# Turning the last layer of a four-layer image kernel: channels on the partitions

## The reference, cut to what matters

```
def _L3_conv_ref(X, Ws, Wm, bm):            # X = _gn(x), L(v, i) = v @ Ws[i-1]
    ...
    ret = L(X, 10) + L(X.transpose(0, 2, 1, 3), 11)
    ret = ret + (L(sum_of_rows, 6) + L(sum_of_cols, 8) + L(diag_part, 12))[:, :, None, :]
    ret = ret + (L(sum_of_rows, 7) + L(sum_of_cols, 9) + L(diag_part, 13))[:, None, :, :]
    ret = ret + 2.0 * L(sum_diag_part, 14)[:, None, None, :]
    ...
    ret = ret + diag_term[:, :, None, :] * eye[None, :, :, None]
    return jax.nn.relu(ret @ Wm + bm)
...
x = x + _L3_conv_ref(_gn(x), L3_conv_Ws, L3_conv_Wm, L3_conv_bm)
```

## Time and profile before

| | |
|---|---|
| median of 3 runs | 1138.73 us (1138.61 to 1141.44) |
| the profiled execution, its span | 1140.7 us |
| busy over the span: PE, DVE, ACT, POOL | 92%, 67%, 43%, 35% |
| end of layer 2 to the first instruction of the block of layer 3 | about 1081.9 to 1086.08 us |
| from there to the first of 16 steps on DVE | 12.7 us |
| 16 steps on DVE | 1098.74 to 1138.25 us |

### The profile page before, as it was taken

One profiled execution on the slowest core, in us unless ns is written; L12 is line 12 of the kernel. 1 busy time (PEld: TensorE's weight loads), 2 busy tenths in 40 slices (PEclk: granted clock), 3 DMA queues, 4 the chain that ended last, 5 costly groups with the idle time before them and its releaser, 6 DMA issues. The chain is left out here.

```text
span 1140.7 us, 25192 instructions
## 1 busy us (share of the span) xinstructions
PE 1047.0 (92%) x9258; PEld 761.3 (67%) x9258; DVE 761.1 (67%) x3620; ACT 490.8 (43%) x1083; POOL 402.6 (35%) x545
## 2 busy tenths in 40 slices
PE   5888999999998699669999999999999999999788
PEld 3435888888887243347677776777777777777576
DVE  3684888888887332366767667676676766766268
ACT  2384777777776100224343343433434343343200
POOL 0153666666665100012232333323233232332331
PEclk8797999999999799769999999999999999999979
DMA  8000000000000000000000000000000000000012
GB/s 171 1 0 2 2 3 3 2 4 2 3 3 2 1 1 1 10 0 1 1 2 1 2 1 1 1 1 2 1 1 2 1 1 1 1 1 1 1 41 111
DMA packets 10317, 11.02 MB, mean 10 GB/s; under 512 B 3668, under 2 KB 8020, under 8 KB 10196
## 3 DMA queue, kind: packets, MB, share of 16 engines
q1 hardware_dynamic: 8820, 8.84, 3.0%
q10 hardware_dynamic: 1376, 0.59, 0.3%
HBM read 5.14 MB, written 4.19 MB: 8 GB/s over the span
## 5 line engine op out<-in xcount | busy, mean ns | idle before, releaser
L1591 PE MATMUL quad<-theta,nat 128*128 128x512 f32 x512 | 240.8, 593 | 0.0
L734 POOL TENSOR_TENSOR nat<-nat,arena 128x512 f32<-128x512 f32 x128 | 131.5, 1049 | 43.7 <-DVE arena L792 39.9
L1599 PEld LDWEIGHTS quad<-flat 128*128 128x128 f32 x768 | 104.7, 190 | 54.5 <-ACT flat L1397 31.7
L1599 PE MATMUL quad<-flat 128*128 128x128 f32 x768 | 123.7, 284 | 9.5 <-ACT flat L1397 9.5
L1591 PEld LDWEIGHTS quad<-theta,nat 128*128 128x128 f32 x512 | 87.5, 191 | 61.7 <-issue 61.7
L792 DVE CUSTOM_DVE_ANT_0 nat<-quad,arena 128x128 f32<-128x128 f32 x512 | 111.2, 283 | 1.9 <-PE quad L878 1.9
L1397 ACT ACTIVATE flat<-quad 128x256 f32<-128x256 f32 x192 | 73.4, 382 | 75.2 <-PE quad L1599 60.5
L751 ACT ACTIVATE nat<-bank 128x512 f32<-128x512 f32 x128 | 73.0, 597 | 65.5 <-PE bank L886 65.5
L1358 POOL COPY img<-flat 64x256 f32<-64x256 f32 x64 | 25.3, 395 | 193.9 <-DVE nat L1502 178.0
L886 PE MATMUL bank<-const,nat 128*128 128x128 f32 x512 | 73.3, 276 | 8.7 <-ACT nat L751 8.0
L756 ACT ACTIVATE nat<-nat 128x512 f32<-128x512 f32 x128 | 77.2, 634 | 4.7 <-POOL nat L734 4.7
(11 more groups left out here) (391 smaller groups left out, 2338.6 us busy)
## 6 DMA issues: line engine op xcount, KB each, us to landing
out<-nat SPq DMA_DIRECT2D x16, 256.0 KB, 2.0
const<-in_constants ACTq DMA_DIRECT2D x1, 400.5 KB, 3.2
arena<-in_L_conv_Ws SPq DMA_DIRECT2D x1, 240.0 KB
flat<-arena SPq DMA_DIRECT2D x3, 32.0 KB, 4.4
nat<-in_x SPq DMA_DIRECT2D x4, 0.2 KB, 12.1
arena<-in_L_conv_Wq ACTq DMA_DIRECT2D x1, 32.0 KB, 6.5
arena<-in_L_conv_Wk ACTq DMA_DIRECT2D x1, 32.0 KB, 6.3
arena<-in_L_conv_Wv ACTq DMA_DIRECT2D x1, 32.0 KB, 6.0
```

The source lines that it names most:

```text
L734: pool.tensor_tensor(scored, scored, of_head(least[b], h).broadcast_to([128, ROWS, L]), ALU.subtract).then_inc(lowered, 1)
L1591: return pe.matmul(m.quad[:, n, :], vT[:, col(n)], m.theta[:, part, :], start=(part == 0), stop=False, skip_group_check=True)
L1599: last = pe.matmul(m.quad[:, row, place * C:(place + 2) * C], a8[g % 2][:, col(row)], zs[half][k % 2][:, n, :], start=False, stop=(k == 2) ...
```

## The change

The layout of layer 3 is turned. Channels are on the partitions, of even columns j in partitions 0 to 63 and of odd ones in 64 to 127; rows i lie along the free axis. `mix` (128 x 64) is the stationary operand and the image the moving one, 512 columns at a time. What hangs on j is then a scalar of each partition, what hangs on i a row. The result is turned back at the end by transposes. In the order of the program:

- `group_norm` gets `sp_aside`: eight transfers from SBUF to SBUF on SP's queue, which copy partitions 0 to 63 of `img` (x itself) to the free tile `flat`, even columns to its lower half and odd ones to its upper half. `raw_rows` on DVE gets two copies, two sums and a scaling more; `sums_of_cols` on POOL drops two operations and clears `diag_pair`.
- The splitting, the three transfers, POOL's conversions and the products with ones are gone, and so are the diagonal tiles.
- The small sums are now 18 matmuls of 128 columns and 12 of one column, with 64 x 64 stationary pieces (before: 15 of 64 columns, two small ones for `both`).
- A step: PE makes 2 matmuls of 512 columns into one of four banks (`mixed`, each into one half of the partitions); DVE 4 scalar_tensor_tensor of 128 columns, then one small tensor_tensor of 128 x 8 on the diagonal; ACT the relu in place; POOL adds x (`residual(t)`, 128 x 512); PE turns the tile by 4 transposes (`turn`); ACT copies it to SBUF; SP sends it. The tiles `work` form a ring of 6, the outgoing ones a ring of 4.

The core of the diff:

```diff
+            for dst, src, landed in sp_aside:
+                sp.dma_start(dst, src).then_inc(landed, 16)
...
+    PARTS = ((0, 2), (2, 6), (6, 11), (11, 16))
+    residual_loads = [(m.flat[halves[q], first * CH:end * CH].rearrange("p (s i) -> p s i", i=L),
+                       stacked[halves[0], first * HALF:end * HALF, q, :], image_in[n])
+                      for n, (first, end) in enumerate(PARTS) for q in range(2)]
...
-    group_norm(nc, m, 3, pool_aside=sums_of_cols, dve_aside=raw_rows)
+    group_norm(nc, m, 3, pool_aside=sums_of_cols, dve_aside=raw_rows, sp_aside=residual_loads)
...
         @block.gpsimd
-            pool.wait_ge(S("flattened"), 16 * 3)
             for t in range(STEPS3):
-                pool.tensor_copy(m.parts[t % 2][:, :], s_flat[:, t * COLS * C:(t + 1) * COLS * C]).then_inc(parts_ready, 1)
+                pool.wait_ge(bent, t + 1)
+                pool.tensor_tensor(w, w, residual(t), ALU.add).then_inc(x_added, 1)
...
         @block.vector
-                dve.tensor_tensor(by_col(before[b]), result(b)[:, :, 0:C], of_row.unsqueeze(1).broadcast_to([128, COLS, C]),
-                                  ALU.add).then_inc(added, 1)
-                dve.tensor_tensor(before[b][own, :], before[b][own, :], diag_tile[t % 4][own, :], ALU.add).then_inc(added, 1)
-                dve.scalar_tensor_tensor(out=by_col(ready[b]), in0=by_col(before[b]), scalar=0.0, in1=result(b)[:, :, C:2 * C],
-                                         op0=ALU.max, op1=ALU.add).then_inc(out_ready, 1)
+                for s in range(HALF):
+                    last = dve.scalar_tensor_tensor(out=w[:, at], in0=m.quad[:, t % 4, at], scalar=of_col[:, t * HALF + s:t * HALF + s + 1],
+                                                    in1=of_row, op0=ALU.add, op1=ALU.add)
+                dve.tensor_tensor(own, own, diag_pair[:, t * HALF:(t + 1) * HALF, :], ALU.add).then_inc(added, 1)
...
+        @block.scalar
+            def keep(t):
+                act.wait_ge(turned, t + 1)
+                if t >= 4:
+                    act.wait_ge(sent[t % 4], 16 * (t // 4))
+                act.activation(ready[t % 4], turned_bank[t % 4][:, :], ACT.Copy).then_inc(out_ready, 1)
+            for t in range(STEPS3 + 3):
+                if t < STEPS3:
+                    act.wait_ge(added, 2 * t + 2)
+                    act.activation(work[t % RING], work[t % RING], ACT.Relu).then_inc(bent, 1)
+                if t >= 3:
+                    keep(t - 3)
...
         @block.tensor
+            def mixed(t):
+                for q in range(2):
+                    last = pe.matmul(m.quad[halves[q], t % 4, :], mix, stacked[:, t * HALF:(t + 1) * HALF, q, :],
+                                     start=True, stop=True, skip_group_check=True)
+            for t in range(0, STEPS3, 2):
+                turn(t)
+                turn(t + 1)
+                for later in (t + 4, t + 5):
+                    if later < STEPS3:
+                        mixed(later)
```

More of the change, by code:

```diff
@@ L8 @@
 F32 = mybir.dt.float32
-BF16 = mybir.dt.bfloat16
 ALU = mybir.AluOpType
@@ L1743, in layer3 @@
[L1743 to L1746, removed]
-    S = lambda name: m.sem(f"l3_{name}")
-    B = m.bank
-    kind = lambda k: w[:, (k - 1) * C:k * C]
-    by_col = lambda t: t.rearrange("p (j x) -> p j x", j=COLS)
+    HALF = COLS // 2
+    RING = 6
+    wm, bm = m.k3_wm, m.k3_bm
+    mix_raw, mix = m.take(C), m.take(C)
@@ new lines, in layer3 @@
+    raw, seen = (m.take(3 * L, C) for _ in range(2))
+    rows_raw, cols_raw, diag_raw = (raw[:, n * L:(n + 1) * L] for n in range(3))
+    rows_x, cols_x, diag_x = (seen[:, n * L:(n + 1) * L] for n in range(3))
+    mean_raw, mean = m.take(3, C), m.take(4, C)
+    col_half = m.take(L)
+    of_row, of_col, level = m.take(L), m.take(L // 2), m.take(2)
+    diag_pair = m.take(L).rearrange("p (s q) -> p s q", q=2)
+    nat_tiles = iter(m.nat[:, n:n + CH] for n in range(0, L * C, CH))
+    work = [next(nat_tiles) for _ in range(RING)]
@@ new lines, in layer3, with residual @@
+    ready = [next(nat_tiles) for _ in range(4)]
+    B = m.bank
+    totals, diag_totals = B[0], B[1]
+    turned_bank = [B[2], B[3], B[0], B[1]]
+    halves = (slice(0, C), slice(C, 128))
+    kind = lambda k: m.k3_w[:, (k - 1) * C:k * C]
+    by_col = lambda t: t.rearrange("p (s x) -> p s x", s=HALF)
+    stacked = m.img[:, 0:L * L].rearrange("p (s q i) -> p s q i", q=2, i=L)
+    def residual(t):
+        return m.flat[:, t * CH:(t + 1) * CH]
+    S = lambda name: m.sem(f"l3_{name}")
+    image_in = [m.sem(f"image_part_in_{n}") for n in range(4)]
@@ L1822, in _ @@
-            dve.wait_ge(terms_made, 4)
-            dve.tensor_copy(diag_term, B[0][:, 0:C]).then_inc(S("diag_ready"), 1)
-            dve.wait_ge(S("diag_ready"), 1)
-            step(lay_diag(dve, 0))
+            step(dve.tensor_copy(level[:, 1:2], diag_totals[:, L:L + 1]))
+            for q in range(2):
+                last = dve.tensor_scalar(diag_pair[halves[q], :, q], diag_totals[halves[q], q:L:2], level[halves[q], 1:2], None, ALU.add)
+            last.then_inc(prepared, 1)
+            dve.wait_ge(prepared, 4)
@@ new lines, in _ @@
+            last.then_inc(terms_made, 1)
+            for q in range(2):
+                total(diag_totals, q, column(0), [(kind(1), diag_x), (kind(3), rows_x), (kind(4), cols_x)])
+            for q in range(2):
+                last = total(diag_totals, q, slice(L, L + 1), [(kind(2), mean[:, 1:2]), (kind(5), mean[:, 0:1])])
+            last.then_inc(terms_made, 1)
+            for t in range(1, 4):
+                mixed(t)
+            for t in range(0, STEPS3, 2):
[4 more added lines that the diff above has]
+                        mixed(later)
@@ L1894, in _ @@
-            for b in range(2):
-                sp.wait_ge(sent[b], 16 * STEPS3 // 2)
+                sp.dma_start(out.rearrange("b i j c -> (b i) j c")[:, t * COLS:(t + 1) * COLS, :],
+                             ready[t % 4].rearrange("p (j c) -> p j c", c=C)).then_inc(sent[t % 4], 16)
+            for n in range(4):
+                sp.wait_ge(sent[n], 16 * (STEPS3 // 4))
 def build(nc, args, out):
```

152 lines of the change are left out of this document (56 added, 96 removed).

## The result

The changed kernel takes 1147.57 us (median of 6 runs, 1145.14 to 1152.26), the kernel before 1138.67 us in the same comparison (6 runs, 1137.71 to 1141.44). The ratio is 1.0074 with an interval of 1.0056 to 1.0092, so the change costs 6.4 to 10.5 us. The profiled execution has a span of 1144.1 us.

A forecast was written before the change was run, and what follows sets the result against it. PE was taken to bound the steps at 2.30 us each. Span 1140.7 plus 10.0 of delay less 5.3 gained gives 1145.4 us, and with the profiled span 2.0 above the median, 1143.4 us; range 1133 to 1149.

The forecast's parts named there:

- The delay: Last block's start: SP hands over eight transfers before the barrier, so it begins 10 us later, ends 4.5 to 13.4.
- the seam: Norm of layer 3 up to the last block's first instruction: 4 us before, to be lengthened by SP's hold.
- The price per run: Eight copies ahead of the barrier: a cost per run and byte, 28 ns for 512 bytes, gives 10.4 us.
- Rival 2: At the barrier: SP doesn't hold the block, issues cost 0.64 us each, time 1134.7 us; chance 0.12 alone.
- Ahead of the steps: Last block's start to its first step: 12.5 us, ends 10 to 13.5, against 12.7 before, so worth nothing.
- The period: Each of the 16 steps: 1.99 us instead of 2.30, because DVE's small operation waits for POOL's sum.
- The ring: In each step: small operation 0.17, relu 0.64, POOL's sum 1.05 and hand-overs form a closed wait of 1.99 us.
- Rival 1: In the steps: no collision on DVE, period 1.6 to 1.7 us, time 1138.5 us; chance 0.15 alone.
- rival 3: In the steps: PE becomes the bound, halves not overlapping or clock low, time 1148 us; chance 0.16 together with rival 4.
- rival 4: In the steps: transfers slower than any row, POOL waits for its parts, above 1147 us; chance 0.16 together with rival 3.
- The tail: After the last step: relu 0.7, sum 1.1, transposes 0.7, copy 0.6, transfer 2.4, in all 5.5 us.
- The sum: Whole kernel: 1140.7 + 10.0 - 5.3 = 1145.4 us of span, thus 1143.4 us of time.

The follow-up runs named there:

- experiments 6 to 8: Changed kernel with its eight copies, in turn, reading both partition halves, reading contiguous sources, or spanning all 128 partitions: 1148.60, 1145.31 and 1144.86 us, one run each.
- experiment 8: Changed kernel with each of the eight copies spread over all 128 partitions on both sides, still in 512-byte runs: 1144.86 us (one run).
- Experiment 1: Changed kernel with the eight copies issued at the head of SP's part of the last block: 1133.48 us, ratio 0.9926 to the kernel before.
- experiment 2: Changed kernel with the small diagonal operation made on the product in PSUM, ahead of the four others: 1141.86 us, ratio 1.0001 to the kernel before.
- experiments 1, 3 and 4: Changed kernel with copies issued in the last block; plus the diagonal added in PSUM; plus eight outgoing tiles: 1133.48, 1131.97 and 1128.59 us.
- Experiment 5: Changed kernel with copies in the last block, diagonal in PSUM, eight outgoing tiles and four thrown-away full-array PE products in the norm: 1130.12 us, ratio 0.9892 to before.
- experiment 3: Changed kernel with both the copies issued in the last block and the diagonal added in PSUM: 1131.97 us, ratio 0.9916 to the kernel before.

## Why the prediction was right, and where not

The measured 1147.57 us lie in the range of 1133 to 1149 around 1143.4, and the kernel became slower, the outcome with the highest chance. The mechanism is the one forecast: SP's transfers hold the barrier, and the small operation waits for POOL's sum. The sizes were met less well, and some of them by luck. Point by point:

- **The delay: right in kind, 3.4 us too small.** I took 10 us of 4.5 to 13.4, and the seam grew by 13.4, the end of my range. SP was held for 16.7 us against some 13.8 in my sum, and 0.7 us passed to the block against 0.3. Behind the hold stand two errors against each other. The rate was 190 GB/s, under the 242 that I had read from a load into 64 partitions; why these copies are slower than that load no run shows. And I let 3.3 MB move before SP comes free, with the queue 0.25 MB ahead of the data; 2.9 MB had moved, so it was some 0.6 MB ahead. At 190 GB/s my 3.3 MB would have given an estimated 18.4 us of hold and a delay of 14.6, beyond my range. That the measured 13.4 stands at its very end is luck: that end came from 206 GB/s. I had weighed runs against partitions and set the value between the two; experiments 6 to 8 speak for the partitions. The price per run isn't wrong by itself: for all 128 partitions it gives an estimated 293 GB/s (16 engines, 28 ns for 512 bytes), and experiment 8 shows 283. But it didn't hold for transfers of 64 partitions.
- **Experiment 1 shows that the place is the cause.** The same transfers behind the barrier leave the seam at 4.8 us. Rival 2, that SP doesn't hold the block, is refuted by after's 16.7 us and by this.
- **Ahead of the steps: 10.1 instead of 12.5 us.** The terms that were mis-sized are those of PE's passes. `mixed(0)` was done 2.3 us into the block where I had 2.9, and the first sums came at 6.9 us where I had 9.4:

```profile
1096.23 1.98 PE L1859 MATMUL quad<-img,arena 128*64 128x512 f32 x4 [14.69 <-DVE arena L1802]
1098.13 3.10 PE L1852 MATMUL bank<-arena 64*64 64x128 f32 x25
```

  The second line holds 23 of the 24 records of 128 columns of the first sums and two of one column: 3.10 us for 25 are 0.12 each, where I had 0.19 to 0.25, though the clock did not rise at all. The starts of the single records in the trace show why: they form two interleaved series of 12, as many as the program has for each half of the partitions, with 0.21 us from one record to the next in each series. So the price of one series was right, and what I had left out is that two halves of the array work side by side here too. The records of one column came 0.11 to 0.17 us apart, near the 0.13 that I had counted.
- **The period: 2.05 us where 1.99 was forecast, through two errors that nearly cancel.** POOL's sum takes 1.26 us, not 1.04: the prediction has the two rows wrong. By the program the row at 1.04 has an operand that holds one value for each 128 columns, and so isn't plain; the one that I put aside (1.27) adds a matrix of 128 columns, over and over, and was the fit. Against that the small operation doesn't add its 0.17 us behind POOL's end but ends 0.03 us after it. The ring is 0.03 + 0.63 + 0.08 + 1.27 + 0.03 = 2.04 us; in three of 14 steps POOL starts 0.06 us later, which gives 2.05 in the mean. Rival 1, no collision, is refuted by the 0.96 us of the median; experiment 2 shows that it would have been worth 7.4 us of the steps, not 5.
- **The halves of PE's array overlap for 512 columns**, against rival 3: 8 records in 1.94 us are 0.24 each, where one after another they take 0.446. PE was busy 20.1 of 28 us in the steps at clock 1.00, as expected:

```profile
1110.00:1138.00 28.00, 20.10 (x106) 8.77 (x104) 27.51 (x68) 14.13 (x26) 17.64 (x14) 1.00 0.27 103
```

- **POOL never waits for the copies**, against rival 4: its first sum comes at 1108.16, and in experiments 1, 3 and 4, where copies and steps overlap, all of its idle time ends with ACT's relu.
- **The tail: 6.0 instead of 5.5 us.** POOL's sum is 0.2 of it, the rest lies in the gaps.
- **The sum.** The single terms are off in both directions: +3.4 - 2.4 + 0.8 + 0.5 = 2.3 on top of my +4.7 gives the measured +7.0. The time lies another 1.9 us above that, by medians (8.9). That a time stands beside its span within a few tenths, as the section on the time before has it, is wrong: in the comparisons a run's time lies about 2 us above its span (1146.23 for 1144.1). So before's profiled execution, with a span of 1140.7, was one of its slower ones, at an estimated 1143 us. The forecast starts from before's median all the same and isn't moved by that. The 7.0 us lie inside the interval of 6.4 to 10.5. What the layers ahead add from one execution to the next is of that size: in profiles of code that is the same up to there the norm of layer 3 begins between 1077.2 and 1083.2. What makes that spread isn't settled.

Slower or faster hung on one number, the time that SP is held, which no row of before showed for a copy of this kind. The layout's own gain was 5.3 us in the forecast and 6.4 measured; that the two are near is luck too, with 2.4 us too much ahead of the steps and 1.3 too little in steps and tail. With the transfers behind the barrier it wins (experiment 1).

## What to carry to other kernels

A DMA-issuing engine is not free once it issues several large transfers in a row: here the first two issues took 0.7 us each and the last three 3.2 to 3.9, and SP came free when 2.9 of 4.2 MB had moved. So large transfers belong behind a barrier and not ahead of it, unless their data time is covered there. A tiny DVE operation with both operands in SBUF can last nearly as long as POOL's operation beside it (0.96 us in the median here against 0.17 alone); with one operand and the output in PSUM it took 0.17. When two changes free time together, look at what had been hidden by the slower version: here the first outputs then queued behind the copies, and a ring of four tiles was too short by one landing of 10 us.

## What the runs showed of the hardware

- **The clock of PE.** Before, it rose from 0.50 to 1.00 (1.2 to 2.4 GHz) 7 us after the block's beginning; in every version with the new layout it stayed at 0.50 for 12 us or more, though PE was as busy. First before, then after (columns of the earlier trace rows):

```profile
1086.00:1093.00 7.00, 6.33 (x30) 6.02 (x31) 4.16 (x20) 0.00 (x0) 0.00 (x0) 0.50 0.06 14
1093.00:1098.00 5.00, 5.00 (x42) 4.54 (x40) 0.45 (x2) 0.00 (x0) 1.16 (x2) 1.00 0.01 3
```

```profile
1096.00:1108.00 12.00, 11.77 (x72) 8.12 (x74) 4.59 (x19) 0.62 (x1) 0.00 (x0) 0.50 0.47 96
```

  What differs in PE's rows is that the new passes use a quarter or a half of the array (64 x 64, 128 x 64). Experiment 5 didn't raise the clock with 4.4 us of full-array work ahead of them. That the small pieces are the cause is not shown: nothing was run with the same passes on the full array, and in experiment 1 the clock rose at 1099.0, while PE still worked on pieces of 128 x 64. The stake is, as an estimate, up to half of the 9.8 us that PE works in the piece ahead.
- **A transfer on a busy queue.** An output tile that lands after 2.0 us landed after 10.0 us with copies ahead of it in the queue (experiment 3).
- **Copies inside SBUF.** 190 GB/s between 64 and 64 partitions in runs of 512 bytes, 283 with 128 partitions in each transfer. In both cases SP came free when 2.9 MB of 4.2 had moved.
- **POOL's sum** of two plain SBUF tiles of 128 x 512 takes 1.26 us, against 1.04 where one operand holds a single value for each 128 columns (line 1374 in the earlier trace rows).
